# The sum over the second FFN's routed experts moves from VectorE to GpSimd, and the work order is planned again

## The reference, cut to what matters

```python
x = x + cross_attention_0(layernorm(x), ctx, ctx)       # 32 query heads, 8 key heads
x = x + ffn_0(layernorm(x))                             # 2 experts, hidden 1024, top 1
x = x + cross_attention_1(layernorm(x), ctx)            # 16 heads, causal
x = x + ffn_1(layernorm(x))                             # 8 routed experts, top 2, a shared expert, a core path
```

```python
h = x @ down_w + down_b                                 # 256 -> 128
gate = softmax of the two largest of softmax(x @ router_w + router_b - cost)
for e in 8 experts:                                     # hidden 128, 256, 384, 512, twice
    out += gate[e] * (expert_e(h) - expert_e(0)) + ...  # GELU, GELU; rows not routed see expert_e(0)
out += 0.1 * shared(h)
out = out @ up_w + up_b + gelu(x) @ core_w + core_b
```

## Time and profile before

| | us |
|---|---|
| three runs, median (lowest to highest) | 364.07 (361.49 to 364.35) |
| the profiled execution, its own time | 360.21 |
| its span, first to last instruction | 358.4 |
| mean granted clock of TensorE in it | 0.976 |
| PE busy | 329.3 |
| DVE busy | 218.9 |
| ACT busy | 161.2 |
| POOL busy | 105.6 |

### The profile page before, as it was taken

The page is one execution under the profiler, slowest core; times in us unless marked ns, Lnnn a source line. Parts: engine busy times, 40 slices in busy tenths (PEclk is TensorE's granted clock), DMA queues, the critical chain, the costliest instruction groups (busy, mean ns, idle before and its releaser), DMA issues.

```text
span 358.4 us, 8192 instructions
## 1 busy us (share of the span) xinstructions
PE 329.3 (92%) x3260; PEld 270.2 (75%) x3260; DVE 218.9 (61%) x566; ACT 161.2 (45%) x345; POOL 105.6 (29%) x190
## 2 busy tenths in 40 slices
PE   0977599999999899999999999899998999998896
PEld 0655477887887788778789688787886887886783
DVE  7789887988897415738257747327373566437235
ACT  1576742557433324441143721445524455445550
POOL 7795315342148512242252271123300000200000
PEclk9968869999999999999999999999999999999999
DMA  8999914336342300034500088300607000300300
GB/s 174 407 379 311 144 30 89 60 59 119 61 81 38 60 2 2 2 60 82 96 4 2 2 190 164 121 2 2 118 2 146 3 2 29 123 0 15 134 0 29
DMA packets 62997, 29.95 MB, mean 84 GB/s; under 512 B 58672, under 2 KB 61040, under 8 KB 61680
## 3 DMA queue, kind: packets, MB, share of 16 engines
q1 hardware_dynamic: 62960, 29.43, 34.1%
HBM read 14.71 MB, written 1.08 MB: 44 GB/s over the span
## 4 chain that ended last, share of the span: by engine, by line
PE 78%; DVE 15%; issue 2%; ACT 2%; DMA 1%; POOL 1%; DVEq 0%; POOLq 0%
PE Y L1352 26%; PE H L1352 23%; PE S L1352 19%; PE S L1397 4%; PE S L1421 2%; DVE MN L1124 2%; DVE PT L1125 2%; DMA QT_OT<-KQS 1%; PE S L1430 1%; PE S L1508 1%; DVE KS L1305 1%; DVE KQS L1184 1%; PE S L1360 1%; DVE K L1111 1%; DVE MN L1131 1%
## 5 line engine op out<-in xcount | busy, mean ns | idle before, releaser
L1352 PE MATMUL H<-XT,WF 128*128 128x256 f32 x256 | 62.7, 392 | 0.0
L1352 PE MATMUL Y<-WP,A 128*128 128x256 f32 x256 | 60.6, 383 | 0.0
L1005 POOL TENSOR_TENSOR A<-R 128x512 f32<-128x512 f32 x32 | 33.5, 1049 | 83.0 <-ACT R L861 79.2
L1352 PEld LDWEIGHTS H<-XT,WF 128*128 128x128 f32 x256 | 48.0, 195 | 6.6 <-issue 0.2
L1352 PEld LDWEIGHTS Y<-WP,A 128*128 128x128 f32 x256 | 47.0, 190 | 6.9 <-issue 0.9
L889 ACT ACTIVATE A<-H,B 128x256 f32<-128x256 f32 x84 | 35.5, 471 | 35.4 <-PE H L1352 35.2
L1352 PE MATMUL Y<-A,W 128*128 128x256 f32 x168 | 44.0, 386 | 0.4 <-DVE KS L1305 0.3
L1352 PE MATMUL H<-CD,W 128*128 128x256 f32 x168 | 42.3, 381 | 0.7 <-ACT CD L878 0.7
L861 ACT ACTIVATE R<-H 128x512 f32<-128x512 f32 x32 | 19.0, 597 | 43.5 <-PE H L1352 43.5
L1305 DVE SCALAR_TENSOR_TENSOR KS<-Y,Y0n,PT 128x256 f32<-128x256 f32 x32 | 15.5, 484 | 33.6 <-PE Y L1352 33.3
L1352 PEld LDWEIGHTS Y<-A,W 128*128 128x128 f32 x168 | 30.8, 190 | 6.5 <-ACT A L889 1.6
(11 more groups left out here) (185 smaller groups left out, 547.5 us busy)
## 6 DMA issues: line engine op xcount, KB each, us to landing
PT<-gates SPq DMA_DIRECT2D x4, 1024.0 KB, 5.4
W<-in_w SPq DMA_DIRECT2D x2, 1344.0 KB, 10.9
WF<-in_wf SPq DMA_DIRECT2D x2, 1024.0 KB, 7.4
WP<-in_wp SPq DMA_DIRECT2D x2, 1024.0 KB, 9.5
X<-in_x SPq DMA_DIRECT2D x8, 128.0 KB, 8.1
out_dram<-X SPq DMA_DIRECT2D x8, 128.0 KB, 1.7
CD<-in_ctx_in SPq DMA_DIRECT2D x2, 256.0 KB, 5.4
C<-in_ctx_in SPq DMA_DIRECT2D x1, 256.0 KB, 3.0
```

The costliest lines, as they stand in the source:

```text
L1005: nc.gpsimd.tensor_tensor(flat(A0[:, n % 2, :, :]), R0[:, n % 2, :], R0[:, n % 2, :], ALU.mult).then_inc(a0_ready, 1)
L1352: return nc.tensor.matmul(o, a, b, start=start, stop=stop, skip_group_check=shared)
```

## The change

POOL adds up `YG`, DVE keeps the product. `YG` keeps its two buffers, now counted through all groups, and a semaphore `yg_used` counts POOL's sums: DVE waits before a product until the sum two before it is done; POOL waits after each sum until it is written; PE's `o` and the DMA of the gates (`gb`, from the third group on) wait on it in place of `acc_ready`.

With it come other inputs to the planner: the cost of `y` (DVE 0.86 becomes DVE 0.48 and POOL 0.72), a factor `COLD` of 1.6 on PE's costs before `WARM` = 28 us, and new values of `SWITCH`, `CHANGE`, `SLACK` and of every priority in `URGENCY`. So besides `y` any step may stand at another place.

```diff
@@ -81,7 +81,7 @@
                  u="pe 1.73 act .6 pool 1.05", d="pe 1.73", y="dve 1.0"),
     "ffn1": dict(v="dve 1.53 pool .7", ln="dve .77", x="pe .45 act .59", i="pool 1.43", r="pe .9 dve .59",
                  e="act .2 dve 1.5", t="act .2 dve 1.2", d="pe .87 act 1.13", g="pe .2 act .27", gd="sp .5", gb="sp .5", c="pe .86 act .94",
-                 w="pe .43", y="dve .86", o="pe 1.3 dve .42", st="sp .5", b="act .22", zp="pool 12.0", z="pe 1.8 dve .16")}
+                 w="pe .43", y="dve .48 pool .72", o="pe 1.3 dve .42", st="sp .5", b="act .22", zp="pool 12.0", z="pe 1.8 dve .16")}
 COST = {part: {s: [(e, float(d)) for e, d in zip(text.split()[::2], text.split()[1::2])] for s, text in costs.items()}
         for part, costs in COST.items()}
 LOADED = {("attn1", "k"): 28.0, ("attn0", "tq"): 28.0, ("attn0", "tk"): 28.0, ("attn0", "c"): 4.6, ("attn0", "b"): 12.0, ("ffn0", "u"): 23.0, ("attn1", "kv"): 9.0, ("ffn1", "z"): 33.0,
@@ -92,27 +92,28 @@
 TABLE_LOAD = 1.3
 TILED = {("attn0", "k"), ("attn0", "s"), ("attn0", "o"), ("attn1", "kv"), ("attn1", "s"), ("attn1", "p"), ("attn1", "o")}
 MODE_CHANGE = 0.09
-SWITCH = 4675.9
-CHANGE = 50
-SLACK = {"act": 0.012, "dve": 0.508, "pe": 0.073, "pool": 0.8, "sp": 0.43}
+WARM, COLD = 28.0, 1.6
+SWITCH = 5323.1
+CHANGE = 183.9
+SLACK = {"act": 0.152, "dve": 0.65, "pe": 0.001, "pool": 0.662, "sp": 0.508}
 GELU = {("ffn1", s) for s in "bdc"}
 EXP = {("attn0", "e"), ("attn1", "p"), ("ffn0", "g"), ("ffn1", "e"), ("ffn1", "t")}
 URGENCY = {
...
 }
 URGENCY = {part: {w[0]: (float(w[1]), float(w[2])) for w in zip(*[iter(text.split())] * 3)} for part, text in URGENCY.items()}
 BODIES = [("ffn0", g) for g in range(GROUPS)] + [("ffn1", g) for g in range(GROUPS)]
@@ -380,6 +381,7 @@
                 d += TABLE_LOAD
             table = mine
         if e == "pe":
+            d *= COLD if at < WARM else 1.0
             now = (s[0], s[2]) in TILED
             d += MODE_CHANGE * (now != tiled)
             tiled = now
@@ -642,7 +644,7 @@
         ld_gates = sem("ld_gates")
         gx_ready = sem("gx_ready")
         gb1_ready = sem("gb1_ready")
-        acc_ready = sem("acc_ready")
+        yg_used = sem("yg_used")
         stored = sem("stored")
         biased = sem("biased")
         zeros_ready = sem("zeros_ready")
@@ -755,7 +757,7 @@
                 sp.wait_ge(gates_kept, 16 * (g + 1))
                 if g >= 2:
 
-                    sp.wait_ge(acc_ready, g - 1)
+                    sp.wait_ge(yg_used, E1 * (g - 1))
                 sp.dma_start(GALL[:, g % 2, 0:E1 * GT], GD[g, :, :].rearrange("e r -> (e r)").unsqueeze(0).to_broadcast(
                     [P, E1 * GT])).then_inc(ld_gates, 16)
 
@@ -977,6 +979,16 @@
                 pool.wait_ge(xn_ready, 2 * TURNS.index(("ffn1", g, "x", 0)) + 2)
                 for t in (2 * g, 2 * g + 1):
                     nc.gpsimd.tensor_tensor(X[:, t, :], X[:, t, :], BR[:, 0, :], ALU.add).then_inc(biased, 1)
+
+            def expert(g, j):
+                if j == 0:
+                    return
+                if j == 1:
+                    read_out(pool, "ffn1", g, "y", 0)
+                n = g * E1 + j - 1
+                read_out(pool, "ffn1", g, "y", j)
+                nc.gpsimd.tensor_tensor(ACC[:, :], ACC[:, :], YG[:, n % 2, :], ALU.add).then_inc(yg_used, 1)
+                pool.wait_ge(yg_used, n + 1)
 
             def zero_products(*_):
 
@@ -1047,7 +1059,7 @@
             run("pool", {("const", "i"): identity_and_ones, ("const", "m"): masks, ("const", "g"): earlier_ones, ("const", "z"): zeros0,
                          ("attn0", "c"): keys0, ("attn0", "v"): norm("attn0"), ("attn1", "v"): norm("attn1"),
                          ("ffn0", "v"): norm("ffn0"), ("ffn1", "v"): norm("ffn1"), ("attn1", "kv"): keys1,
-                         ("ffn1", "i"): biases, ("ffn1", "zp"): zero_products, ("ffn0", "u"): square})
+                         ("ffn1", "i"): biases, ("ffn1", "zp"): zero_products, ("ffn1", "y"): expert, ("ffn0", "u"): square})
 
 
         @block.vector
@@ -1298,18 +1310,15 @@
                 if j == 0:
                     return
                 if j == 1:
-                    read_out(dve, "ffn1", g, "y", 0)
                     dve.wait_ge(ld_gates, 16 * (g + 1))
+                n = g * E1 + j - 1
+                if n >= 2:
+
+                    dve.wait_ge(yg_used, n - 1)
                 e = EXPERTS[j]
                 b, done = filled(dve, "ffn1", g, "y", j)
-                nc.vector.scalar_tensor_tensor(YG[:, j % 2, :], b[:, 0:GT], Y0n[:, e:e + 1],
+                nc.vector.scalar_tensor_tensor(YG[:, n % 2, :], b[:, 0:GT], Y0n[:, e:e + 1],
                                                GALL[:, g % 2, e * GT:(e + 1) * GT], ALU.add, ALU.mult).then_inc(done, 1)
-                read_out(dve, "ffn1", g, "y", j)
-                add = nc.vector.tensor_tensor(ACC[:, :], ACC[:, :], YG[:, j % 2, :], ALU.add)
-                if j < E1:
-                    link(add)
-                else:
-                    add.then_inc(acc_ready, 1)
 
             def result_ffn1(g, k):
 
@@ -1599,7 +1608,7 @@
                 for dc in range(DC):
                     mm(b[:, 0:D], GX[:, dc, k * P:(k + 1) * P], CW[:, dc, :], start=(dc == 0), stop=False)
                 if k == 0:
-                    pe.wait_ge(acc_ready, g + 1)
+                    pe.wait_ge(yg_used, E1 * (g + 1))
                 mm(b[:, 0:D], ACC[:, k * P:(k + 1) * P], UW[:, :], start=False).then_inc(done, 1)
 
 
```

## The result

The changed kernel took 367.0 us (median of 4 runs, 366.46 to 367.15), the kernel before beside it 362.78 (median of 4, 360.36 to 364.35); the ratio is 1.0162, 95% interval 1.0102 to 1.0222. It is **slower** by more than the 1% that the prediction took for no change, where 3.8 us less was forecast: 5.9 us by the ratio, 4.2 by the medians. The ratios of this document compare fast runs alone, which leaves out 28 of the 75 later runs of the kernel before (they span 358.60 to 369.99 us), so that they are not the quotients of the medians (here 1.0116).

What follows compares the result with a forecast made beforehand. PE was taken as the bound, busy 329.3 of 358.4 us. Terms -0.6 - 0.2 + 0.1 + 0.1 - 2.1 - 1.1 = -3.8 took 360.21 to 356.4, plus 3.86 for the median: 360.3 us, range 353 to 369.5.

Steps and rivals of the forecast that it cites:

- The addition: Sums leave DVE (13.6 us less) for POOL (24.1 us more); counted at nothing except at three places.
- Place 1: Queries of attention 1 in the first group's tail: PE's 0.82 us wait for turned queries shrinks, -0.6 us.
- Place 2: Last group's gates: PE's 2.42 us wait for them shrinks by 0 to 0.43 us, taken as -0.2.
- Place 3: Tail: POOL adds up the last four experts one after the other, +0.1 us, bounds -0.3 to +0.5.
- The new waits: Products waiting for the sum two before cost nothing as long as POOL comes to its additions in time.
- rival C: POOL's slower queue takes the place of DVE's, so DVE and then PE wait: 370.4 us, chance 0.22.
- B: Rival: the sums were hidden in DVE's gaps, and the order's gains are lost to the ports: 364 us, chance 0.19.
- Ports: DVE and POOL hinder each other in some pairs of instructions: +0.1 us, 0 to 2.9 over four groups.
- The new plan at the start: Planner may put first scores ahead of attention 1's keys and values: -2.1 us, bounds -4.3 to +2.8.
- PE's idle time from 10 to 50 us: Sign at the start: should fall below 9.4 us; the forecast is wrong if PE's idle time there grows.
- The new plan elsewhere: New order removes or makes waits like the two for the gates: -1.1 us, between -3.4 and +3.4.
- the clock: Sign of being wrong: PE's busy time changes by several us because the clock falls elsewhere; no price given.

Runs made afterwards that it cites:

- e10: Changed kernel's new order, but the sums left on DVE and the first group's gates load issued late; ratio 1.0129 to the kernel before.
- e1: Kernel before with only the sums moved to POOL, every engine keeping its old order; ratio 0.9979 to the kernel before.
- e3: Changed kernel with the first group's 1 MB gates load held back until PE has turned back tile 3 of attention 1; ratio 0.999 to the kernel before.
- e7: Changed kernel with the old order up to the planned 60 us, the new order after it, and the late gates load; ratio 1.0022 to the kernel before.
- e9: Changed kernel with the late gates load and PE's step of eight wide matmuls put ahead of the 128 short ones; ratio 1.0024 to the kernel before.
- e11: Changed kernel with the old order up to 60 us, late gates load, and eight wide matmuls ahead of the short ones; ratio 1.0021 to the kernel before.
- e2: Kernel before with the changed kernel's order on every engine, sums still on DVE, gates load early; ratio 1.0193 to the kernel before.
- e6: Changed kernel with the late gates load plus an extra load of the same 1 MB at the old time; ratio 1.0159 to the kernel before.
- e8: The changed kernel timed a second time, nothing altered; 367.05 us, ratio 1.0162 to the kernel before.
- e5: Changed kernel, gates load early, with PE's step of eight wide matmuls put ahead of the 128 short ones; ratio 1.007 to the kernel before.
- h2: Changed kernel with the new order up to the planned 60 us and the old order for the rest; ratio 1.0101 to the kernel before.

## Why the prediction was wrong

*The addition, places 1 to 3.* About right in the order of before; in the new order it was worth more (e10). DVE's busy time fell by 13.8 us and POOL's rose by 23.0. The groups of DVE and POOL in the changed kernel, against the earlier trace rows:

```profile
L990 POOL TENSOR_TENSOR KS<-KS 128x256 f32<-128x256 f32 x32 | 23.2, 726 | 69.3 <-DVE KS L1320 68.7
...
L1320 DVE SCALAR_TENSOR_TENSOR KS<-Y,Y0n,PT 128x256 f32<-128x256 f32 x32 | 15.3, 484 | 39.6 <-PE Y L1361 37.3
```

Place 1, forecast at -0.6: -0.5 in the order of before (e1), and -1.0 at its neighbour `XA` in the new order (e3 against e10). Place 2, forecast at -0.2: nothing, 2.43 us for 2.42. Place 3, forecast at +0.1: in the changed kernel's chain the last chain of sums goes as worked out,

```profile
356.96 0.50 DVE KS L1320
...
357.59 0.74 POOL KS L990
...
359.98 2.01 PE Y L1361 x8
```

359.98 - 356.96 = 3.02 us from product to `UW`, where the earlier trace rows have 353.74 - 350.79 = 2.95.

Where the clock in the tail is as before (e1, e7, e9) it takes 21.08 to 21.11 us from the last gates to `UW`, against 21.03 before: +0.1, as forecast.

*The new waits, and rival C.* DVE waited 2.3 us for POOL in all, and PE 0.85, in the tail. Rival C fell, though its time, 370.4, was the nearest but one to the result: a right-looking number from a mechanism that didn't happen. B's 364 was nearest, by ports that take what the order wins, and neither happened.

*Ports.* Nothing: the product takes 484 ns as before, XN 503 ns on average where it was 512. The +0.1 and its bound of 2.9 were not needed.

*The new plan at the start, -2.1.* Wrong. The start of PE in the changed kernel, against the earlier trace rows:

```profile
10.54 3.78 PE L1361 MATMUL S<-WKV,CT 64*128 64x512 f32 x4
...
16.06 0.64 PE L1361 MATMUL H<-K,QT 128*64 128x128 bf16 x8
```

Keys and values of attention 1 even stand a step earlier than before, ahead of the second half of the first queries, and the first scores still begin at 16.06. I took the factor of 1.6 for a hint that scores would come first. It worked the other way: the changed kernel's planner, with the factor set to 1, puts PE's first nine steps as before; with 1.6 it moves keys and values forward. (A slip in the working: half of ACT's 1.93 us from 10.75 on is 11.72, not 11.76; the bound of 4.3 stands.) PE's idle time from 10 to 50 us, 9.4 in the earlier trace rows, is 40 - (9.12 + 7.08 + 5.09 + 7.05) = 11.7:

```profile
10.00:20.00 10.00, 9.12 (x90) 5.70 (x88) 9.16 (x23) 7.83 (x17) 8.22 (x24) 1.00 0.99 412
20.00:30.00 10.00, 7.08 (x108) 5.04 (x102) 9.69 (x16) 6.90 (x13) 8.41 (x16) 1.00 1.06 390
30.00:40.00 10.00, 5.09 (x92) 3.98 (x92) 8.85 (x24) 8.30 (x14) 4.41 (x14) 1.00 1.19 212
40.00:50.00 10.00, 7.05 (x29) 5.85 (x30) 8.29 (x21) 4.75 (x10) 2.07 (x6) 0.57 0.34 64
```

The prediction had named that as a sign of being wrong. But it isn't the loss: the traces of the experiments have PE busy 27.5 to 30.2 us of these 40 with the new start (nine kernels) and 25.9 to 30.6 with the old one (the kernel before, e1, e7 and e11), with other clocks in it. And PE comes to its run of `PT,V` at 202.13 to 203.96 with the new start (the changed kernel, e2, e3, e6, e8, e10), and at 204.26 with the old start and the same rest (e7).

*The new plan elsewhere, -1.1.* **This is the step that failed.** It was bounded at 3.4 us either way by waits for data that the old trace shows. The loss came from a wait that the old trace has only as 0.5 us of "issue", and from a clock that fell behind it: 3.5 to 4.6 us in one stretch (10.07 us in the changed kernel, 9.02 in e8 and 9.94 in e6 against 5.50 in e3). The prediction priced PE's waits for other engines and no wait of PE for its own instructions; the clock it named only as a sign of being wrong, at no price. The mechanism is shown as far as this: the stop stands at a fixed place in the list (e5), its length follows the traffic of the DMA engines (e3, e6), and the loss goes with it. That the 16 KB packet of the instruction queue is what PE waits for is inferred, from its times: in ten traces PE goes on 1.4 to 1.5 us after it ends. It is its beginning that the traffic delays: from the first matmul of the burst it takes 3.67 us in the changed kernel (201.00 to 204.67), 3.37 in e6 (202.12 to 205.49) and 1.50 in e3 (202.80 to 204.30). The 2.17 us between the changed kernel and e3 are the 2.20 by which the stop is longer. Why the packet begins when the load ends no run shows. On such packets the Trainium skill ("Runtime: NRT & Kernel Launch", section "Instruction fetch mechanics") says that each sequencer fetches its instructions in pages of 16 KiB by a DMA queue of its own, and that crossing a page is mostly hidden. The packet agrees with the first half; the stops of 1.18 and 3.38 us show that here it was not hidden.

*The sum.* Forecast -3.8, measured +5.9 by the ratio, a difference of 9.7: 2.1 of the start and 1.1 of the other waits that weren't won, and the 3.5 to 4.6 of this stretch, 6.7 to 7.8 in all. The other 1.9 to 3.0 are about the interval of the ratio (0.6% of 363 us is 2.2); by the medians, +4.2, the difference is 8.0 and next to nothing is left. In the two traces 1.4 us more stand in the tail: from the last group's gates to `UW` it is 22.44 us in the changed kernel and 21.03 before. The wait of PE ahead of it is the same (2.43 and 2.42 us), but behind it the granted clock is 0.82 to 0.83 in the windows from 335 to 345 of the changed kernel, and 1.00 before. This is not what the late load takes away: e3 has 22.43 as well.

## What to carry to other kernels

When an order is planned again, read it not only for which wait ends last but for what the DMA engines do beside the densest run of short instructions: a large load whose time isn't tight should not start there. A wait that the profile puts down to "issue" and that moves with the instruction count, not with the step, is told from a data wait by moving a few instructions in front of it. And price a stop of PE at what follows too: the clock behind it about doubled the cost here. The late load takes the loss away and no more: no kernel tried here is clearly faster than the one before.

## What was not expected of the hardware

Stops of this kind are there without such traffic too (1.18 and 0.94 us in e3 and e7 at a DMA share of 0.02 or less, 0.53 among other `PT,V` matmuls in the kernel before), and the one of the new order grows to 3.1 to 3.4 us beside a load of 1 MB that takes 5.1 us from issue to landing.

The granted clock fell behind all four stops of 3.1 to 3.4 us (0.52, 0.67, 0.72 and 0.86 in the window from 205 to 210 of the changed kernel, e2, e6 and e8), and behind none of 1.57 us and less (1.00 in e1, e3, e5, e7, e10 and h2). Behind waits of about 2.4 us it did either: 0.79 after 2.37 us in e2, 1.00 after 2.38 in e10. The plainest case is one wait that all thirteen traces have, 2.42 to 2.43 us for the last group's gates. In six (the changed kernel, e2, e3, e6, e8, e11) the clock fell behind it, and the tail from there to `UW` took 22.38 to 22.47 us; in seven (the kernel before, e1, e5, e7, e9, e10, h2) it stayed at 1.00, and the tail took 21.03 to 21.11. The same wait costs 1.3 us more or not, and nothing here shows what decides it.
